# Two grouped attentions of a decoder: value products issued in pairs, output products two units behind

## The chip, the cores and the metric

The kernel runs on one core of a Trainium2 chip. The metric is the device time of one execution in microseconds; the profiler gives, for one execution, what each engine did and when. TensorE (PE) multiplies, with its weight loads shown apart (PEld); VectorE (DVE) and ScalarE (ACT) read and write both the accumulator banks (PSUM) and on-chip memory (SBUF); GpSimd (POOL) here splits weights; SyncE (SP) issues DMAs.

## What is computed

Two decoder layers with layer norms behind each block, on x of 16 x 64 tokens and 512 features, in float32. The change touches the two blocks with 32 heads of 128 and 8 key/value heads (four query heads share one):

```python
# block B: cross attention, layer 0: keys and values from ctx, rotary embedding, mask
q = rope(x @ Wq); k = rope(ctx @ Wk); v = ctx @ Wv
o = softmax(where(mask == 0, -1e9, q @ k.T / sqrt(128))) @ v
x = layernorm(x + o @ Wo)
# block D: self attention, layer 1: causal, window of 64
o = softmax(where(causal, q @ k.T / sqrt(128), -inf)) @ v
x = layernorm(x + o @ wo.T)
```

The blocks before, between and behind them (another attention, two feed-forward blocks, a single-head cross attention) are not changed.

## The kernel before, in words

Tokens lie in 8 tiles (NT) of 128, that is two batch rows of 64 each. `grouped_attention` (line 685) is called for B (line 1097, with rotation) and for D (line 1250, without). Either works through four parts; a part is a pair of key/value heads. A part has 16 units (SLOTS): unit u is token tile u % 8 with key/value head u // 8 of the pair, so it holds 2 batch rows x 4 query heads. The first three parts run in a hardware loop, the last one (`part.final`) is written out behind it. Each engine runs its own instruction stream; semaphores with running counts order them.

Matrix products with weights are made from high and low parts: `three` (line 88) gives high x high, high x low and low x high, and `product` (line 80) accumulates them in one bank. So each activation has to be split before it is multiplied: ScalarE writes the high part, VectorE subtracts it from the bank to get the low part.

On TensorE, slot u does in this order (`turn`, line 852):

- T(u): two transposes of unit u's probabilities into bankT (line 858), when VectorE has them ready (`prob`).
- S(u+2): scores of unit u+2 into a bankA (line 825). In late slots (u % 4 == 2) they come further back.
- O(u): the value product. Two matmuls of 64 rows, one for each batch row, into the two banks of bankO (line 870). The trace shows each as two passes, four in all. It waits for ScalarE's copy of T(u) (`pt_done`), for the values, and until bankO has been split for unit u-1 (`o_low`).
- Y(u-1): the output product of the unit before (`output`, line 828), 12 matmuls of 512 columns from oT, the split O, into a bankY. It waits for the low part of oT and for the bank. In late slots it stands ahead of O(u).
- Q(u+6): a query projection, 12 matmuls of 512 columns; in some slots a value projection V, and four key projections K in slot 13. A projection waits until its bankA is drained (in B: until the first rotation step of the query two banks before).
- at u % 8 == 7 also Y(u), its halves counted apart (`wo_used`).

On ScalarE, slot u copies T(u) to pt (line 959), in B copies the two halves of Q(u+5) swapped (line 910) and in D copies Q(u+5) itself (line 912), writes the high part of O(u) to oT (line 967), and then computes exp of unit u+2 (line 922); in late slots that exp comes in the slot behind. In slots of SPLIT_AT it also writes the high part of a weight block (line 937). In the final part it does the first `ln_roots` (line 111; the square roots of tiles 0 to 3, whose table has to be loaded) behind slot 14.

On VectorE, slot u interleaves (`in_turns`) the rotation of Q(u+5) in three steps (lines 1013, 1015, 1019; B alone), the front of the softmax of unit u+2 (lines 1026, 1030, 1033) and the back of unit u+1 (lines 1038, 1041, 1044). Then come the residual of u-2 (line 1049; in the final part with the layer norm's statistics, `ln_follow`), the low part of O(u) (line 1082) and the low part of a weight block (line 1060).

oT is kept twice, by u % 2, and bankO holds one unit in columns 0 to 255 of its two banks:

```python
oT = [[sb(mem, f"{tag}oT{i}{p}", [P, GROUP, 2, S], F32R) for p in range(2)] for i in range(2)]
...
act.wait_ge(o_ready, part.unit(u) + 1)
nc.scalar.activation(oT[u % 2][0][:].rearrange("p h b q -> p b h q"),
                     bankO[:, :, 0:GROUP * S].rearrange("p b (h q) -> p b h q", h=GROUP), ACT.Copy).then_inc(o_high, 1)
if not late(u) and (u + 2 < SLOTS or not part.final):
    exp(part, u + 2)
```

Of the kernel before, what the change touches and what calls it, by code (L numbers as in the profile page):

```python
# [42 lines left out]
def build_program(nc, io):  # L43
# [641 lines left out]
    def grouped_attention(tag, norm, first, source, rope, following):  # L685
# [6 lines left out]
        with ExitStack() as mem:  # L692
# [12 lines left out]
            oT = [[sb(mem, f"{tag}oT{i}{p}", [P, GROUP, 2, S], F32R) for p in range(2)] for i in range(2)]  # L705
# [13 lines left out]
            for i, (q, o) in enumerate(zip(halves(wq, "p h k n -> p (h k n)"), halves(wo, "p h n -> p (h n)"))):  # L719
                dst[f"q{i}"] = dst[f"q{i + 2}"] = q  # L720
                dst[f"o{i}"] = dst[f"o{i + 2}"] = o

# [7 lines left out]
            with nc.Block() as block:  # L730
# [30 lines left out]
                def _(pe):  # L761
# [67 lines left out]
                    def output(part, u):  # L829

                        if u % NT == 0:
                            pe.wait_ge(w_low, part.block("o3" if u else "o1"))
                        pe.wait_ge(o_low, part.unit(u) + 2)
                        pe.wait_ge(y_done, part.unit(u) + 1)
                        pairs = [x for h in range(GROUP) for x in three([o[:, h].rearrange("p b q -> p (b q)") for o in oT[u % 2]], [w[:, h, :] for w in wo])]
                        if u % NT == NT - 1:
                            product(bankY[u % 2][:], pairs[:len(pairs) // 2], stop=False).then_inc(wo_used, 1)
                            product(bankY[u % 2][:], pairs[len(pairs) // 2:], start=False).then_inc(y_ready, 1)
                        else:
                            product(bankY[u % 2][:], pairs).then_inc(y_ready, 1)  # L840

# [10 lines left out]
                    def turn(part):  # L852
                        for u in range(SLOTS):
                            banks = slot_banks(u, part.final)
                            pe.wait_ge(st["prob"], part.unit(u) + 1)
                            pe.wait_ge(pt_done, part.unit(u) + 1)
                            for hp in range(2):
                                done = nc.tensor.transpose(bankT[u % 2][:, hp * P:(hp + 1) * P], sc[u % 4][:, hp].rearrange("p b k -> p (b k)"), ident[:])  # L858
                            done.then_inc(t_ready, 1)
                            if banks and banks[0][0] == "S" and not late(u):  # L860
                                project(part, banks[0])
                            if late(u):
                                output(part, u - 1)
                            if u < NT and u % 2 == 0:
                                pe.wait_ge(v_done, part.it * 4 + u // 2 + 1)
                            pe.wait_ge(pt_done, part.unit(u) + 3)
                            pe.wait_ge(o_low, part.unit(u) + 1)
                            for b in range(2):
                                rows = slice(S * b, S * b + S)
                                done = nc.tensor.matmul(bankO[:, b, 0:GROUP * S], V[rows, u % NT, u // NT * HD:(u // NT + 1) * HD], pt[u % 2][rows, :], start=True, stop=True)  # L870
                            done.then_inc(o_ready, 1)
                            if u % NT and not late(u):
                                output(part, u - 1)
                            for x in banks:
                                if x[0] != "S" or late(u):
                                    project(part, x)
                            if u % NT == NT - 1:
                                output(part, u)
# [20 lines left out]
                def _(act):  # L899
# [50 lines left out]
                    def turn(part):  # L950
                        for u in range(SLOTS):
# [12 lines left out]
                            if len(banks) == 1:  # L964
                                queries_or_keys(part, banks[0])
                            act.wait_ge(o_ready, part.unit(u) + 1)
                            nc.scalar.activation(oT[u % 2][0][:].rearrange("p h b q -> p b h q"),  # L967
                                                 bankO[:, :, 0:GROUP * S].rearrange("p b (h q) -> p b h q", h=GROUP), ACT.Copy).then_inc(o_high, 1)
                            if not late(u) and (u + 2 < SLOTS or not part.final):
                                exp(part, u + 2)  # L970
                            if u in VALUES_AT and not part.final:
# [5 lines left out]
                            if part.final and u == SLOTS - 2:  # L977
                                ln_roots(act, norm + 1, 0)
# [5 lines left out]
                def _(dve):  # L984
# [85 lines left out]
                    def turn(part):  # L1070
                        for u in range(SLOTS):
# [7 lines left out]
                            if u % NT >= 2:  # L1079
                                residual(part, u - 2)  # L1080
                            dve.wait_ge(o_high, part.unit(u) + 1)
                            nc.vector.tensor_tensor(oT[u % 2][1][:].rearrange("p h b q -> p b h q"), bankO[:, :, 0:GROUP * S].rearrange("p b (h q) -> p b h q", h=GROUP),  # L1082
                                                    f32(oT[u % 2][0][:]).rearrange("p h b q -> p b h q"), ALU.subtract).then_inc(o_low, 1)
# [6 lines left out]
                            if u % NT == NT - 1:  # L1090
                                residual(part, u - 1)
# [612 lines left out]
```

## Time and profile before

| | |
|---|---|
| median of 3 runs | 1679.96 us (1678.95 to 1680.19) |
| the profiled execution | 1680.69 us, span 1678.9 us |
| mean granted TensorE clock | 0.984 of 2.4 GHz |
| TensorE busy | 1584.1 us (94% of the span), 8504 matmuls |
| VectorE busy | 983.7 us (59%) |
| ScalarE busy | 657.6 us (39%) |
| GpSimd busy | 202.6 us (12%) |
| block B | about 253 to 801 us |
| block D | about 900 to 1438 us |

Busy time of an engine says how full it is, not what waits for what; TensorE's idle time, and what ended it, shows that. In the rows, a line stands for a group of instructions: start, time, engine, line of the kernel, operation, out<-in, partitions x elements and count; in brackets the idle time of the engine before it and what ended it. Matmuls overlap, so the time from start to start is what one costs, and the time of one is longer.

### The profile page before, as it was taken

What the parts mean: (1) busy time and instruction counts of PE and PEld (TensorE: products, weight loads), DVE (VectorE), ACT (ScalarE), POOL (GpSimd) and SP (SyncE); (2) the same over time, 40 slices, a digit from 0 to 9 for tenths busy, and PEclk for the clock granted to TensorE, in tenths of its full rate; (3) what the DMA queues carried; (4) which work ended last, traced back from release to release, by engine and by line L of the source; (5) the groups of instructions that cost most, each with busy time, mean ns of one, the idle gap of its engine ahead of it and who ended that gap; (6) DMA issues with size and microseconds to landing.
All of it is one profiled execution on the core that took longest, in us unless ns stands there. A gap on an engine that the chain in (4) does not pass through costs nothing. (4 is left out here: it accounts for less than half of the span.)

```text
span 1678.9 us, 22758 instructions
## 1 busy us (share of the span) xinstructions
PE 1584.1 (94%) x8504; PEld 1269.8 (76%) x8504; DVE 983.7 (59%) x1948; ACT 657.6 (39%) x1193; POOL 202.6 (12%) x146
## 2 busy tenths in 40 slices
PE   8688799999999999999889999999999999989998
PEld 6566587787788778776777788788878877767876
DVE  5997767756766776677433542452553346246655
ACT  4476434333433443433233322332332323426541
POOL 8321130000000000000340000000000000703330
PEclk9899999999999999999999999999999999999999
DMA  6011011101110110100111110110110100202231
GB/s 229 30 38 40 15 49 63 51 13 39 38 51 2 63 51 13 39 13 26 45 52 38 41 48 13 50 51 12 50 60 15 38 13 25 77 10 77 77 90 50
DMA packets 26023, 75.44 MB, mean 45 GB/s; under 512 B 3888, under 2 KB 4624, under 8 KB 25680
## 3 DMA queue, kind: packets, MB, share of 16 engines
q1 hardware_dynamic: 25552, 73.16, 13.2%
q8 instruction: 63, 1.03, 0.2%
q0 software_dynamic: 384, 1.05, 0.2%
q14 instruction: 24, 0.20, 0.0%
HBM read 72.10 MB, written 2.10 MB: 44 GB/s over the span
## 5 line engine op out<-in xcount | busy, mean ns | idle before, releaser
L83 PE MATMUL bankY<-sb_Dwo,sb_DoT 128*128 128x512 f32 x768 | 194.0, 402 | 0.3 <-DVE sb_DoT L1082 0.3
L83 PE MATMUL bankY<-sb_Bwo,sb_BoT 128*128 128x512 f32 x768 | 193.0, 400 | 0.2 <-DVE sb_BoT L1082 0.2
L83 PE MATMUL bankA<-sb_xT,sb_Bwq 128*128 128x512 f32 x768 | 190.4, 397 | 0.9 <-issue 0.9
L83 PE MATMUL bankA<-sb_xT,sb_Dwq 128*128 128x512 f32 x768 | 189.9, 396 | 0.0
L83 PEld LDWEIGHTS bankY<-sb_Dwo,sb_DoT 128*128 128x128 f32 x768 | 141.0, 189 | 42.3 <-issue 13.3
L83 PEld LDWEIGHTS bankY<-sb_Bwo,sb_BoT 128*128 128x128 f32 x768 | 140.6, 189 | 42.0 <-issue 13.2
L83 PEld LDWEIGHTS bankA<-sb_xT,sb_Bwq 128*128 128x128 f32 x768 | 142.3, 188 | 35.2 <-issue 4.0
L83 PEld LDWEIGHTS bankA<-sb_xT,sb_Dwq 128*128 128x128 f32 x768 | 142.2, 188 | 34.0 <-issue 2.7
L1013 DVE TENSOR_TENSOR sb_BqT<-bankA,sb_Btable 128x512 f32<-128x512 f32 x64 | 44.3, 692 | 150.3 <-ACT sb_Bsw L910 150.3
L1049 DVE TENSOR_TENSOR sb_xtok<-sb_xtok,bankY 128x512 f32<-128x512 f32 x128 | 87.2, 681 | 54.0 <-PE bankY L83 53.9
L910 ACT ACTIVATE sb_Bsw<-bankA 64x512 f32<-64x512 f32 x160 | 94.7, 592 | 54.9 <-PE bankA L83 51.7
L1026 DVE TENSOR_TENSOR sb_Dsc<-bankA,sb_Dbound 128x256 f32<-128x256 f32 x64 | 27.0, 421 | 149.2 <-PE bankA L825 149.2
L1082 DVE TENSOR_TENSOR sb_DoT<-bankO,sb_DoT 128x512 fp32r<-128x512 f32 x64 | 43.8, 685 | 117.3 <-ACT sb_DoT L967 117.3
L959 ACT ACTIVATE sb_Dpt<-bankT 128x256 f32<-128x256 f32 x64 | 24.5, 382 | 155.2 <-PE bankT L858 155.2
L825 PE MATMUL bankA<-sb_Bkt,sb_BqT 128*128 128x128 f32 x512 | 69.3, 278 | 8.0 <-DVE sb_BqT L1019 7.8
L78 POOL TENSOR_TENSOR sb_Ew<-sb_raw,sb_zero 128x1024 fp32r<-128x1024 f32 x4 | 7.6, 1891 | 566.3 <-POOLq L730 566.3
L825 PEld LDWEIGHTS bankA<-sb_Bkt,sb_BqT 128*128 128x128 f32 x512 | 62.1, 191 | 14.3 <-DVE sb_BqT L1019 8.7
L922 ACT ACTIVATE sb_Bsc<-sb_Bsc 128x256 f32<-128x256 f32 x64 | 26.7, 416 | 115.5 <-DVE sb_Bsc L1033 115.5
L78 POOL TENSOR_TENSOR sb_Cwar<-sb_raw,sb_zero 128x1024 fp32r<-128x1024 f32 x1 | 1.9, 1892 | 575.8 <-POOLq L730 575.8
L825 PE MATMUL bankA<-sb_Dkt,sb_DqT 128*128 128x128 f32 x512 | 69.0, 278 | 0.0
L825 PEld LDWEIGHTS bankA<-sb_Dkt,sb_DqT 128*128 128x128 f32 x512 | 62.2, 191 | 5.1 <-issue 5.0
L967 ACT ACTIVATE sb_DoT<-bankO 128x512 fp32r<-128x512 f32 x64 | 38.3, 599 | 65.0 <-PE bankO L870 65.0
(277 smaller groups left out, 2968.2 us busy)
## 6 DMA issues: line engine op xcount, KB each, us to landing
sb_raw<-in_w_attn SPq DMA_DIRECT2D x80, 512.0 KB, 3.5
sb_raw<-in_q_gu SPq DMA_DIRECT2D x22, 256.0 KB, 2.7
sb_raw<-in_q_d SPq DMA_DIRECT2D x11, 256.0 KB, 2.7
sb_raw<-in_wqk SPq DMA_DIRECT2D x8, 256.0 KB, 2.6
sb_rawx<-in_xT SPq DMA_DIRECT2D x4, 512.0 KB, 5.7
sb_raw<-in_ctxT SPq DMA_DIRECT2D x4, 512.0 KB, 6.2
sb_xtok<-in_x_tok SPq DMA_DIRECT2D x1, 2048.0 KB, 13.1
sb_raw<-in_ctx_tok SPq DMA_DIRECT2D x4, 512.0 KB, 3.8
```

Of the source, the lines that this page charges most:

```text
L78: return nc.gpsimd.tensor_tensor(dst, src, zero[0:src.shape[0]].to_broadcast([src.shape[0], src.shape[1]]), ALU.add)
L83: last = nc.tensor.matmul(out, lhs, rhs, start=start and i == 0, stop=stop and i == len(pairs) - 1)
L825: done = nc.tensor.matmul(bank[:, at:at + P], qT[:, 2 * t + b, 2 * hp:2 * hp + 2, :].rearrange("p h q -> p (h q)"), window(kt, 2 * t + b, ...
L910: nc.scalar.activation(sw[part.swap(x)][64 * i:64 * i + 64, :], bankA[part.buffer(x)][64 - 64 * i:P - 64 * i, :], ACT.Copy).then_inc(swapp ...
L922: nc.scalar.activation(flat, flat, ACT.Exp, scale=HD ** -0.5).then_inc(st["exp"], 1)
L959: nc.scalar.activation(pt[u % 2][:], bankT[u % 2][:, 0:GROUP * S], ACT.Copy).then_inc(pt_done, 1)
L967: nc.scalar.activation(oT[u % 2][0][:].rearrange("p h b q -> p b h q"), bankO[:, :, 0:GROUP * S].rearrange("p b (h q) -> p b h q", h=GROUP ...
L1013: nc.vector.tensor_tensor(to, bankA[part.buffer(x)][:].rearrange("p (b s) -> p b s", s=S), table[:, 0, half].rearrange("p (b s) -> p b s", ...
L1026: nc.vector.tensor_tensor(s3, bankA[part.buffer(("S", u))][:].rearrange("p (a c) -> p a c", a=2)[:, :, S:S + P], bound_of(u).unsqueeze(1). ...
L1049: nc.vector.tensor_tensor(xtok[:, t, :], xtok[:, t, :], bankY[u % 2][:], ALU.add).then_inc(y_done, 1)
L1082: nc.vector.tensor_tensor(oT[u % 2][1][:].rearrange("p h b q -> p b h q"), bankO[:, :, 0:GROUP * S].rearrange("p b (h q) -> p b h q", h=GR ...
```

## The change

- The value products of two units are issued together, in odd slots: `attend(part, u)` makes O(u-1) and O(u) one behind the other, into columns 0 to 255 (even unit) and 256 to 511 (odd unit) of bankO's two banks. It waits for both copies of transposes and until the pair before has been split.
- oT holds one pair, [P, 2, GROUP, 2, S] for either part, instead of two units apart. One ScalarE instruction writes the high part of the pair and one VectorE instruction its low part (1024 columns instead of twice 512), in odd slots.
- The output product runs two units behind: Y(u-2) in slots with u % 8 >= 2, ahead of the pair's value products; Y(6) and Y(7) at the end of slot 7 (14 and 15 in slot 15). The residual runs three units behind.
- On ScalarE exp(u+2) stands ahead of the high part of O, not behind it.
- In the last slot of the final part the pair is split unit by unit, and Y(13) comes behind the value products. The first `ln_roots` moves from the end of slot 14 to behind the high part of unit 14, ahead of that of unit 15.

```diff
@@ -702,7 +702,7 @@
             V = sb(mem, f"{tag}V", [P, NT, 2 * HD])
             sc = [sb(mem, f"{tag}sc{i}", [P, 2, 2, S]) for i in range(4)]
             pt = [sb(mem, f"{tag}pt{i}", [P, GROUP * S]) for i in range(2)]
-            oT = [[sb(mem, f"{tag}oT{i}{p}", [P, GROUP, 2, S], F32R) for p in range(2)] for i in range(2)]
+            oT = [sb(mem, f"{tag}oT{p}", [P, 2, GROUP, 2, S], F32R) for p in range(2)]
             mx = sb(mem, f"{tag}mx", [P, 2, 4]); sm = sb(mem, f"{tag}sm", [P, 2, 4]); ri = sb(mem, f"{tag}ri", [P, 2, 4])
             if rope:
                 sw = [sb(mem, f"{tag}sw{i}", [P, HALF]) for i in range(2)]
@@ -719,6 +719,18 @@
             for i, (q, o) in enumerate(zip(halves(wq, "p h k n -> p (h k n)"), halves(wo, "p h n -> p (h n)"))):
                 dst[f"q{i}"] = dst[f"q{i + 2}"] = q
                 dst[f"o{i}"] = dst[f"o{i + 2}"] = o
+
+            def side(v):
+                return slice(v % 2 * GROUP * S, (v % 2 + 1) * GROUP * S)
+
+            def of_pair(i):
+                return oT[i][:].rearrange("p v h b q -> p b (v h) q")
+
+            def of_unit(i, v):
+                return oT[i][:, v % 2].rearrange("p h b q -> p b h q")
+
+            pair_bank = bankO[:].rearrange("p b (h q) -> p b h q", q=S)
+            unit_bank = lambda v: bankO[:, :, side(v)].rearrange("p b (h q) -> p b h q", q=S)
 
             def run(engine, start, turn):
 
@@ -832,12 +844,24 @@
                             pe.wait_ge(w_low, part.block("o3" if u else "o1"))
                         pe.wait_ge(o_low, part.unit(u) + 2)
                         pe.wait_ge(y_done, part.unit(u) + 1)
-                        pairs = [x for h in range(GROUP) for x in three([o[:, h].rearrange("p b q -> p (b q)") for o in oT[u % 2]], [w[:, h, :] for w in wo])]
+                        pairs = [x for h in range(GROUP) for x in three([o[:, u % 2, h].rearrange("p b q -> p (b q)") for o in oT], [w[:, h, :] for w in wo])]
                         if u % NT == NT - 1:
                             product(bankY[u % 2][:], pairs[:len(pairs) // 2], stop=False).then_inc(wo_used, 1)
                             product(bankY[u % 2][:], pairs[len(pairs) // 2:], start=False).then_inc(y_ready, 1)
                         else:
                             product(bankY[u % 2][:], pairs).then_inc(y_ready, 1)
+
+                    def attend(part, u):
+
+                        if u < NT:
+                            pe.wait_ge(v_done, part.it * 4 + u // 2 + 1)
+                        pe.wait_ge(pt_done, part.unit(u) + 3)
+                        pe.wait_ge(o_low, part.unit(u))
+                        for v in (u - 1, u):
+                            for b in range(2):
+                                rows = slice(S * b, S * b + S)
+                                done = nc.tensor.matmul(bankO[:, b, side(v)], V[rows, v % NT, v // NT * HD:(v // NT + 1) * HD], pt[v % 2][rows, :], start=True, stop=True)
+                            done.then_inc(o_ready, 1)
 
                     def start(part):
                         if rope:
@@ -859,22 +883,18 @@
                             done.then_inc(t_ready, 1)
                             if banks and banks[0][0] == "S" and not late(u):
                                 project(part, banks[0])
-                            if late(u):
-                                output(part, u - 1)
-                            if u < NT and u % 2 == 0:
-                                pe.wait_ge(v_done, part.it * 4 + u // 2 + 1)
-                            pe.wait_ge(pt_done, part.unit(u) + 3)
-                            pe.wait_ge(o_low, part.unit(u) + 1)
-                            for b in range(2):
-                                rows = slice(S * b, S * b + S)
-                                done = nc.tensor.matmul(bankO[:, b, 0:GROUP * S], V[rows, u % NT, u // NT * HD:(u // NT + 1) * HD], pt[u % 2][rows, :], start=True, stop=True)
-                            done.then_inc(o_ready, 1)
-                            if u % NT and not late(u):
-                                output(part, u - 1)
+                            ending = part.final and u == SLOTS - 1
+                            if u % NT >= 2 and not ending:
+                                output(part, u - 2)
+                            if u % 2:
+                                attend(part, u)
+                            if ending:
+                                output(part, u - 2)
                             for x in banks:
                                 if x[0] != "S" or late(u):
                                     project(part, x)
                             if u % NT == NT - 1:
+                                output(part, u - 1)
                                 output(part, u)
                     run(pe, start, turn)
                     ln_tensor(pe, norm + 1, EARLY)
@@ -963,19 +983,24 @@
                                 exp(part, u + 1)
                             if len(banks) == 1:
                                 queries_or_keys(part, banks[0])
-                            act.wait_ge(o_ready, part.unit(u) + 1)
-                            nc.scalar.activation(oT[u % 2][0][:].rearrange("p h b q -> p b h q"),
-                                                 bankO[:, :, 0:GROUP * S].rearrange("p b (h q) -> p b h q", h=GROUP), ACT.Copy).then_inc(o_high, 1)
                             if not late(u) and (u + 2 < SLOTS or not part.final):
                                 exp(part, u + 2)
+                            if part.final and u == SLOTS - 1:
+                                act.wait_ge(o_ready, part.unit(u) + 1)
+                                nc.scalar.activation(of_unit(0, u - 1), unit_bank(u - 1), ACT.Copy).then_inc(o_high, 1)
+                                ln_roots(act, norm + 1, 0)
+                                act.wait_ge(y_ready, part.unit(u - 2) + 1)
+                                act.wait_ge(o_low, part.unit(u - 1) + 2)
+                                nc.scalar.activation(of_unit(0, u), unit_bank(u), ACT.Copy).then_inc(o_high, 1)
+                            elif u % 2:
+                                act.wait_ge(o_ready, part.unit(u) + 1)
+                                nc.scalar.activation(of_pair(0), pair_bank, ACT.Copy).then_inc(o_high, 2)
                             if u in VALUES_AT and not part.final:
                                 values(part, VALUES_AT[u])
                             if u in SPLIT_AT:
                                 weights_high(part, SPLIT_AT[u])
                             for x in projected_last(u, part.final):
                                 queries_or_keys(part, x)
-                            if part.final and u == SLOTS - 2:
-                                ln_roots(act, norm + 1, 0)
                             if part.final and u == SLOTS - 1:
                                 ln_rest(act, norm + 1)
                     run(act, start, turn)
@@ -1076,11 +1101,15 @@
                             in_turns(rotate(part, *banks) if rope and banks else None,
                                      None if late(u) else scores,
                                      back(part, u + 1) if u + 1 < SLOTS or not part.final else None)
-                            if u % NT >= 2:
-                                residual(part, u - 2)
-                            dve.wait_ge(o_high, part.unit(u) + 1)
-                            nc.vector.tensor_tensor(oT[u % 2][1][:].rearrange("p h b q -> p b h q"), bankO[:, :, 0:GROUP * S].rearrange("p b (h q) -> p b h q", h=GROUP),
-                                                    f32(oT[u % 2][0][:]).rearrange("p h b q -> p b h q"), ALU.subtract).then_inc(o_low, 1)
+                            if u % NT >= 3:
+                                residual(part, u - 3)
+                            if part.final and u == SLOTS - 1:
+                                for v in (u - 1, u):
+                                    dve.wait_ge(o_high, part.unit(v) + 1)
+                                    nc.vector.tensor_tensor(of_unit(1, v), unit_bank(v), f32(of_unit(0, v)), ALU.subtract).then_inc(o_low, 1)
+                            elif u % 2:
+                                dve.wait_ge(o_high, part.unit(u) + 1)
+                                nc.vector.tensor_tensor(of_pair(1), pair_bank, f32(of_pair(0)), ALU.subtract).then_inc(o_low, 2)
                             if u % NT == 0:
                                 weights_low(part, "o3" if u else "o1")
                             if u in SPLIT_AT:
@@ -1088,6 +1117,7 @@
                             if late(u):
                                 in_turns(scores)
                             if u % NT == NT - 1:
+                                residual(part, u - 2)
                                 residual(part, u - 1)
                                 if rope:
                                     in_turns(rotate(part, *projected_last(u, part.final)))
```

## Rows read from the trace of the kernel before

**Rows 1.** Stretches B, D: us, busy PE, PEld, DVE, ACT, POOL, PEclk, DMA share, GB/s.

```profile
253.00:801.00 548.00, 533.20 (x2793) 427.35 (x2793) 377.75 (x776) 220.50 (x393) 0.02 (x1) 1.00 0.11 35
...
900.00:1438.00 538.00, 533.37 (x2795) 427.64 (x2793) 249.99 (x564) 173.83 (x321) 0.00 (x0) 1.00 0.11 35
```

**Rows 2.** Groups by line and shape: busy us, mean ns, idle before, releasers.

```profile
L825 PE MATMUL bankA<-sb_Bkt,sb_BqT 128*128 128x128 f32 x512 | 69.3, 278 | 8.0 <-DVE sb_BqT L1019 7.8 <-DVE sb_BqT L1013 0.2
...
L870 PE MATMUL bankO<-sb_Bpt,sb_BV 64*128 64x256 f32 x256 | 45.5, 432 | 4.6 <-ACT sb_Bpt L959 3.6 <-DVE sb_BoT L1082 1.0
...
L870 PE MATMUL bankO<-sb_Dpt,sb_DV 64*128 64x256 f32 x256 | 45.0, 428 | 3.0 <-ACT sb_Dpt L959 3.0
...
L83 PE MATMUL bankY<-sb_Bwo,sb_BoT 128*128 128x512 f32 x768 | 193.0, 400 | 0.2 <-DVE sb_BoT L1082 0.2
...
L83 PE MATMUL bankY<-sb_Dwo,sb_DoT 128*128 128x512 f32 x768 | 194.0, 402 | 0.3 <-DVE sb_DoT L1082 0.3
```

**Rows 3.** TensorE's timeline, one D unit: start, us, ..., [idle]; last, second half of 907.25.

```profile
906.04 0.38 PE L858 MATMUL bankT<-sb_ident,sb_Dsc 128*128 128x128 f32 x2
906.26 1.06 PE L825 MATMUL bankA<-sb_Dkt,sb_DqT 128*128 128x128 f32 x8
907.25 0.70 PE L870 MATMUL bankO<-sb_Dpt,sb_DV 64*128 64x256 f32 x4
907.88 3.03 PE L83 MATMUL bankY<-sb_Dwo,sb_DoT 128*128 128x512 f32 x12
910.75 2.96 PE L83 MATMUL bankA<-sb_xT,sb_Dwq 128*128 128x512 f32 x12
913.55 0.38 PE L858 MATMUL bankT<-sb_ident,sb_Dsc 128*128 128x128 f32 x2
...
907.57 0.38 PE L870 MATMUL bankO<-sb_Dpt,sb_DV 64*128 64x256 f32 x2
```

**Rows 4.** Timeline of TensorE, B, units 1 and 2 of a part.

```profile
404.37 0.38 PE L858 MATMUL bankT<-sb_ident,sb_Bsc 128*128 128x128 f32 x2
...
411.85 0.38 PE L858 MATMUL bankT<-sb_ident,sb_Bsc 128*128 128x128 f32 x2
411.99 3.01 PE L83 MATMUL bankY<-sb_Bwo,sb_BoT 128*128 128x512 f32 x12
...
416.19 1.16 PE L825 MATMUL bankA<-sb_Bkt,sb_BqT 128*128 128x128 f32 x8 [0.56 <-DVE sb_BqT L1019]
```

**Rows 5.** Timeline of ScalarE and VectorE, B, the same units.

```profile
406.43 0.69 DVE L1013 TENSOR_TENSOR sb_BqT<-bankA,sb_Btable 128x512 f32<-128x512 f32 x1 [1.35 <-ACT sb_Bsw L910]
...
409.69 0.42 DVE L1044 TENSOR_TENSOR sb_Bsc<-sb_Bsc,sb_Bri 128x256 f32<-128x256 f32 x1
...
409.80 0.42 ACT L922 ACTIVATE sb_Bsc<-sb_Bsc 128x256 f32<-128x256 f32 x1 [2.78 <-DVE sb_Bsc L1033]
...
410.13 1.04 ACT L937 ACTIVATE sb_Bwq<-sb_raw 128x1024 fp32r<-128x1024 f32 x1
...
411.20 1.23 DVE L1060 TENSOR_TENSOR sb_Bwq<-sb_raw,sb_Bwq 128x1024 fp32r<-128x1024 f32 x1 [0.50 <-ACT sb_Bwq L937]
```

**Rows 6.** Timeline, the end of D.

```profile
1424.96 1.28 ACT L111 ACT_TABLE_LOAD   x1
...
1426.87 0.70 PE L870 MATMUL bankO<-sb_Dpt,sb_DV 64*128 64x256 f32 x4 [2.21 <-ACT sb_Dpt L959]
...
1427.50 7.39 PE L83 MATMUL bankY<-sb_Dwo,sb_DoT 128*128 128x512 f32 x24
...
1428.11 2.92 ACT L117 ACTIVATE sb_xtok<-sb_xtok,sb_ln_offset,sb_ln_rstd 128x512 f32<-128x512 f32 x4
...
1434.73 1.04 PE L168 MATMUL bankT<-sb_ident,sb_xtok 128*128 128x128 f32 x8
...
1437.33 0.55 DVE L148 TENSOR_SCALAR sb_xtok<-sb_xtok,sb_ln_rstd,sb_ln_offset 128x512 f32<-128x512 f32 x1
```

**Rows 7.** One stretch of the end of D, columns as in rows 1.

```profile
1429.00:1431.00 2.00, 2.00 (x6) 1.54 (x6) 0.00 (x0) 2.00 (x4) 0.00 (x0) 0.50 0.00 0
```

## The prediction, made before the change was timed

> **What bounds the kernel now.** I read first the busy time of the two stretches that the change touches, the cross attention B and the windowed attention D: TensorE is busy for 533.2 of 548 us and 533.4 of 538 us, VectorE for 378 and 250 us [rows 1]. So TensorE's order of work is the time in both, and VectorE has little room in B and much in D. The groups by line show what TensorE waits for: 7.8 us for rotated queries in B, 4.6 and 3.0 us in all before value products, 0.2 and 0.3 before output products [rows 2]. Then the timeline of one ordinary D unit [rows 3], of units 1 and 2 of a part in B on TensorE [rows 4] and on ScalarE and VectorE [rows 5], and of the last units [rows 6]. There the last value product waits 2.21 us for a copy that is queued behind the table load and the square root. The granted clock of one stretch there is in [rows 7].
>
> **Part 1, pairing the value products.** In [rows 3] eight 128-column passes start at 906.26 and the value product at 907.25: 0.99 us where eight at the pace of 0.11 take 0.89, so 0.10 to enter. The product holds TensorE 0.63 us (907.25 to 907.88); its second half starts 0.32 after the first. The following twelve take 2.87 us, the next twelve 2.80; twelve at 0.23 are 2.77, so leaving costs 0.10 more. A pass of 256 columns at the pace above would take 0.22, two of them 0.43: 0.20 of the 0.63 is weight loading at entry and running empty at the exit. One product in the middle of others thus costs 0.83, of which 0.40 is changing over. Paired, the second product costs between 0.43 (only streaming) and 0.63 (as now). I take 0.43, since the 0.32 between the halves is 0.11 of first load plus 0.21, the streaming alone, and a load behind a running pass is hidden everywhere in [rows 3]. 64 pairs x 0.40 = **-25.6 us** (lower bound of the gain 64 x 0.20 = 12.8).
>
> The Trainium skill (TensorEngine Tiling (Array Packing), Key Properties) says that changing the tiling mode drains TensorE. The 0.10, 0.20 and 0.10 agree with it.
>
> **Part 2, one split for both.** The ScalarE copy of 1024 columns takes 1.04 us and the VectorE subtraction 1.22, as the weight blocks of that size do [rows 5]. With three handovers of somewhat under 0.1 the pair's low part is there 2.5 us after the second product. It is less busy time than before, but one later, longer chain, and in ScalarE's order exp(u+2) now stands ahead of the copy, so the copy waits for VectorE's softmax of unit u+2.
>
> **Part 3, what the output product now waits for.** It stands at u-2: at units 1 and 9 there is none, and at unit 2 (10) output(0) needs the pair of units 0 and 1. Count from the transposes of unit 1 in B (404.37) by [rows 4, 5]. VectorE's first rotation step of Q6 ends at +2.75 and frees the bank that Q7 needs; TensorE is ready at 0.22+0.98+0.63+0.43 = 2.26, since output(0) no longer stands between: 0.55 idle. Probabilities of unit 2 are done at +5.74, TensorE ready at 5.68: 0.1. exp(3) runs +5.43 to 5.85, so the pair's copy ends at 6.80 and the subtraction at 8.05; output(0) starts at 8.1 where it could at 6.0: **2.1 idle**. VectorE then has the low part of a weight block (1.2) and Q7's rotation (2.2) before S(4): +11.6, output(0) being over at 11.05: 0.6. That is 3.35 us idle at unit 1 and at unit 9: 8 halves x 3.35 = +26.8. In D there is no rotation: its three steps of 0.7 [rows 5], of which 0.1 lies under the next, are gone from ahead of exp(3), which is over 1.9 us earlier, and the same count leaves 0.25 x 8 = +2.0.
>
> The scores of unit 8 (in slot 6) come at a fixed 4.34 us after the transposes, as at unit 2 (411.85 to 416.19), through copy, swap and rotation, whatever TensorE does meanwhile. The value product that stood there (0.83) is gone, so the 0.6 wait grows to 1.3: 4 x 1.3 = +5.2. By the same chain output(6), now directly behind Q13, waits 0.55 in four parts (+2.2), and the scores of unit 16 wait 0.5 in three (+1.5). The first slot of B, whose Q6 waits for VectorE anyway, gives nothing back: +0.8. The waits that these replace go: 12 in late slots, 0.56 idle and the 0.07 beside it each [rows 4], in all -7.6 of the 7.8 [rows 2].
>
> **Part 4, the last units of B and D.** No projections are left there. At unit 12 only transposes and scores (1.1 us) stand between the pair (10, 11) and output(10), which needs 2.5: 1.35 idle; at unit 14 the transposes alone (0.22): 2.25; at unit 15 the products wait for the copy of their transposes: 0.6. Together +4.2 each, **+8.4**. What stood there goes: the waits at units 11, 12, 14 and 15, in B 1.0 for the low part and 2.2 for the copy before value products, 0.2 before an output product; in D 2.2 and 0.3 [rows 2, 6]: -5.9, D's first product's 0.8 being handed on to the next transposes, which wait for VectorE instead. After the 2.21 wait TensorE ran at a granted clock of 0.50 (1.2 GHz) [rows 7]: 24 output matmuls took 7.23 us (1427.50 to 1434.73) instead of 5.6 [rows 6]; I take 1.5 each: -3.0.
>
> Roots behind the last product: the table load (1.28) and root (0.30) no longer stand ahead of the transposes' copy [rows 6], they lie beside output(13). But tiles 0 to 3 are normalised only after residual(13), which comes behind both last splits, some 3 us later; that pushes the roots and scalings of the groups behind it. Before, the last normalisation ends 3.4 us after output(15) (1434.73 to 1437.88 and its hand-over); worked out with the 4 scalings (2.92 [rows 6]) that would now start 8.2 us after unit 15's transposes, then a root, 2 scalings and the last group, it becomes 4.45: +1.05 x 2 = +2.1.
>
> SyncE and GpSimd: no DMA is added, loads follow the low parts of the weights and have microseconds to spare; no work moves past them. oT needs half the memory, no time.
>
> **Sum.** New waits: 26.8+2.0+5.2+2.2+1.5+0.8+8.4+2.1 = +49.0. Gone: 25.6+7.6+5.9+3.0 = -42.1. Net +6.9 on the profiled execution's 1680.69 (span 1678.9): 1687.6; the median shown is 0.7 lower, so 1686.9. Ten of the new waits are about as long as the one in [rows 6], after which the clock fell. If it falls after two of them, at 1.2 each (a part is absorbed by the wait for S(4)), it is **1689**.
>
> **Rivals.**
> (a) Faster: the cross attention's queue doesn't bind. Mechanism: the pair's copy and subtraction finish under Q7, as they nearly do in D by the count above, and only the saved change-overs count. Place: unit 1 and 9 in B; price: without the 35.7 us of B's waits (26.8+5.2+2.2+1.5), 1651. It decides once B's new waits are under 29 us. For it: VectorE is idle 170 of 548 us in B [rows 1]. Against it: exp(3) starts at 409.80, 5.4 us after the transposes, and the copy is behind it in ScalarE's order. The rule of the Trainium skill named above (TensorEngine Tiling (Array Packing), Key Properties), taken alone, gives this way: half as many changes of mode, so faster. 8%.
> (b) The second product of a pair costs what the first does, 0.63. That adds 0.20 x 64 = 12.8, of which some 3.5 fall into waits: 1698. Against it: the halves' distance. 12%.
> (c) The clock falls at nearly all ten long waits, 8 x 1.0 + 2 x 1.5 = +11: 1698. For it: it fell after the 2.21 wait [rows 6, 7]. Against it: that wait stood between short products and transposes, while twelve full matmuls stand on either side of the new ones. 18%.
> (d) The forecast, 62%.
>
> **How the numbers follow.** The forecast's own range is 1682 to 1694: of 49 us of waits, eight counts of the same chain at unit 1 carry 27, and 0.1 us on the copy or subtraction moves the sum by about 1.5, 0.3 by 4 to 5. The range for 8 in 10 reaches to (b) and (c): 1681 to 1699. A measurement here can tell about 0.2% (3.4 us) from no change. Faster than 1676.6: (a) and a tail of the forecast, 0.09. Between 1676.6 and 1683.3: the lower edge of the forecast, 0.12. Slower: 0.79.
>
> **What would show it.** In the changed kernel's timeline: the value products as groups of 8, about 1.06 us long (1.26 would be (b)); a pair's copy of about 1.04 and subtraction of about 1.22; TensorE idle before output matmuls for the low part of oT, about 2.1 us at units 2 and 10 of B and 0.25 in D; waits for rotated queries grown from 7.8 to over 15 us; the stretch of D some 10 us shorter and that of B some 17 longer. No wait for the copy of the transposes behind the table load. Wrong if B's stretch grows by less than 8 us, if the idle time at unit 2 is under 1 us, or if a wait appears on a weight block.

## The result, and the profile after

The changed kernel takes 1700.7 us (median of 4 runs, 1700.1 to 1705.1), the kernel before 1679.84 (4 runs, 1678.95 to 1680.19): a ratio of 1.0125, interval 1.0113 to 1.0137. It is slower, as forecast, but by 20.9 us where the forecast had 9, and 1.7 us beyond the end of the range. The profiled execution took 1700.43 us, span 1698.5, mean granted clock 0.977 (before 0.984).

First the two stretches of [rows 1], from the same events to the same events, in the columns of [rows 1].

```profile
253.00:827.00 574.00, 537.45 (x2795) 432.20 (x2793) 380.44 (x748) 212.26 (x361) 0.00 (x0) 0.98 0.10 34
926.00:1456.00 530.00, 521.88 (x2796) 426.91 (x2794) 250.52 (x533) 168.29 (x290) 0.00 (x0) 1.00 0.11 36
```

B is 26 us longer and D 8 shorter. In B TensorE's busy time grew by 4 us although change-overs were removed, and the mean clock fell to 0.98: idle time and a slower clock both have a share. The groups by line and shape of the changed kernel (busy us, mean ns, idle before and its releasers) say where TensorE now stands idle.

```profile
L83 PE MATMUL bankY<-sb_Bwo,sb_BoT 128*128 128x512 f32 x768 | 199.8, 413 | 20.7 <-issue 15.7 <-DVE sb_BoT L1112 5.0
L83 PE MATMUL bankY<-sb_Dwo,sb_DoT 128*128 128x512 f32 x768 | 190.1, 398 | 4.2 <-DVE sb_DoT L1112 3.4
L837 PE MATMUL bankA<-sb_Bkt,sb_BqT 128*128 128x128 f32 x512 | 69.3, 279 | 7.6 <-DVE sb_BqT L1044 5.8 <-DVE sb_Bkt L1044 1.6 <-DVE sb_BqT L1038 0.2
L863 PE MATMUL bankO<-sb_Bpt,sb_BV 64*128 64x256 f32 x256 | 36.3, 402 | 0.5 <-ACT sb_Bpt L979 0.5
L863 PE MATMUL bankO<-sb_Dpt,sb_DV 64*128 64x256 f32 x256 | 36.3, 402 | 0.5 <-ACT sb_Dpt L979 0.5
```

Against [rows 2]: the value products wait 0.5 us in a block where they waited 4.6 and 3.0, and are busy 9 us less in each block; B's output products wait 20.7 us where they waited 0.2, and a single one of their matmuls takes 413 ns on average against 398 in D. Eight of these waits, 15.7 us in all and 2.0 at most, are put down to "issue".

TensorE's timeline of B, the units of [rows 4] (start, us, engine, line, operation, tiles, number, [idle before]):

```profile
411.24 0.38 PE L882 MATMUL bankT<-sb_ident,sb_Bsc 128*128 128x128 f32 x2
411.46 1.06 PE L837 MATMUL bankA<-sb_Bkt,sb_BqT 128*128 128x128 f32 x8
412.45 1.13 PE L863 MATMUL bankO<-sb_Bpt,sb_BV 64*128 64x256 f32 x8
414.06 3.04 PE L83 MATMUL bankA<-sb_xT,sb_Bwq 128*128 128x512 f32 x12 [0.47 <-DVE sb_BqT L1038]
417.04 0.44 PE L882 MATMUL bankT<-sb_ident,sb_Bsc 128*128 128x128 f32 x2
419.44 4.57 PE L83 MATMUL bankY<-sb_Bwo,sb_BoT 128*128 128x512 f32 x12 [1.96 <-issue]
423.85 0.38 PE L837 MATMUL bankA<-sb_Bkt,sb_BqT 128*128 128x128 f32 x2
```

Timeline of ScalarE and VectorE for the same units, as in [rows 5]:

```profile
416.68 0.42 ACT L942 ACTIVATE sb_Bsc<-sb_Bsc 128x256 f32<-128x256 f32 x1 [3.40 <-DVE sb_Bsc L1058]
417.00 1.00 ACT L997 ACTIVATE sb_BoT<-bankO 128x1024 fp32r<-128x1024 f32 x1
...
418.11 1.23 DVE L1112 TENSOR_TENSOR sb_BoT<-bankO,sb_BoT 128x1024 fp32r<-128x1024 f32 x1 [1.13 <-ACT sb_BoT L997]
```

The pair's value products are over at 413.5, but ScalarE takes exp(3) first, at 416.68, 5.44 us after the transposes, and the copy behind it. The subtraction ends at 419.34 and output(0) starts at 419.44: TensorE has stood still since 417.48. "Issue" is this same wait for the low part of oT, though the view doesn't name it: all eight are 1.96 us long, and each ends 0.1 us after a subtraction has. And the twelve matmuls behind it take 4.41 us (419.44 to 423.85) where [rows 3] have 2.87. The granted clock says why; two windows of the changed kernel, columns as in [rows 1]:

```profile
417.00:419.50 2.50, 0.54 (x4) 0.29 (x3) 1.39 (x2) 2.48 (x5) 0.00 (x0) 1.00 0.00 0
419.50:423.00 3.50, 3.50 (x10) 2.75 (x11) 3.44 (x7) 0.94 (x2) 0.00 (x0) 0.58 0.34 117
```

The clock is full (2.4 GHz) up to the wait's end and 0.58 on the mean behind it: most of that stretch ran at 1.2 GHz. Distances from one unit's transposes to the next ones', worked out from the two timelines for the second part of B, units 0 to 15, show which units pay for it:

```
before  5.39 7.48  8.13 7.50 7.49 7.49 8.12 10.26 4.72 7.48 11.01 7.49 10.35 18.38 10.35 13.10
after   4.00 5.80 10.50 7.91 6.66 7.89 8.14 14.04 3.91 5.80 13.37 7.89  9.52 18.81 10.32 16.47
```

Unit 2 is 10.50 in the first two parts and 9.53 and 9.58 in the other two; unit 10 is 13.37 in three parts and 7.70 in the last; unit 14 of the last parts is 7.04 (B) and 7.02 (D). So the clock fell at eight of the ten long waits: twice at unit 2, four times at unit 10, twice at unit 14. Against the same units with the clock full (9.53 at unit 2 here; 12.39 and, in the last part, 6.13 at unit 10 in experiment 3) a fall costs 1.0 us at each of five places and 1.6 at the last unit 10. At the two units 14 no run has the full clock; an estimate (the output product starts 2.58 us behind the transposes, and twelve matmuls at full clock take 2.8) makes them 5.4, and the fall some 1.7 each. That is 9.8 us in all, against some 3, by the prediction's count, that the kernel before had lost in the same way at its two units 15.

In D nothing of the kind happens in the looped parts. TensorE there, units 1 and 2 of the first part (the last row output(0)):

```profile
931.83 1.06 PE L837 MATMUL bankA<-sb_Dkt,sb_DqT 128*128 128x128 f32 x8
932.82 1.13 PE L863 MATMUL bankO<-sb_Dpt,sb_DV 64*128 64x256 f32 x8
933.88 3.05 PE L83 MATMUL bankA<-sb_xT,sb_Dwq 128*128 128x512 f32 x12
936.77 0.38 PE L882 MATMUL bankT<-sb_ident,sb_Dsc 128*128 128x128 f32 x2
937.26 2.97 PE L83 MATMUL bankY<-sb_Dwo,sb_DoT 128*128 128x512 f32 x12
```

The pair lasts 1.06 us (932.82 to 933.88), and output(0) comes 0.27 us after the transposes are through (936.77 + 0.22). At the end of D, however, both waits of the last units are there:

```profile
1434.16 0.44 PE L882 MATMUL bankT<-sb_ident,sb_Dsc 128*128 128x128 f32 x2
1436.74 4.60 PE L83 MATMUL bankY<-sb_Dwo,sb_DoT 128*128 128x512 f32 x12 [2.14 <-DVE sb_DoT L1112]
1441.18 0.38 PE L882 MATMUL bankT<-sb_ident,sb_Dsc 128*128 128x128 f32 x2
1442.04 1.14 PE L863 MATMUL bankO<-sb_Dpt,sb_DV 64*128 64x256 f32 x8 [0.47 <-ACT sb_Dpt L979]
```

The 2.21 us of [rows 6] have become 0.47, but a wait of 2.14 stands one unit earlier in the order of work, and the clock falls behind that one instead (4.60 us for twelve matmuls).

Where the 19.6 us of span went, from the starts of the blocks' parts in both traces: B's three looped parts +19.4 (145.78, 144.76, 144.74 before; 153.25, 151.04, 150.44 after), B's last part +5.5 up to its last transposes, its tail up to the last tiles' layer norm +1.0, D's looped parts -8.4, D's last part -1.0, its tail +0.9. The rest, 2.2, lies in stretches whose code the change leaves alone: 0.8 ahead of B, -0.4 between the blocks, 1.8 behind D.

The 1.8 behind D is a fall of the clock too. TensorE waits there for the last tiles' layer norm, 1.80 us before and 2.93 after, because the norm is over later. The 10 us from that wait's end, first in the kernel before and then in the changed one, columns as in [rows 1]:

```profile
1438.40:1448.40 10.00, 7.88 (x41) 6.32 (x42) 4.88 (x8) 4.71 (x9) 9.81 (x5) 1.00 0.20 63
1456.20:1466.20 10.00, 8.55 (x32) 6.87 (x33) 4.88 (x8) 4.67 (x9) 9.79 (x5) 0.66 0.19 65
```

All of the 1.8 us is lost in these 10 us. In every run with pairs in D's last part (the change, experiments 1, 2 and 3) the wait is 2.93 and the clock 0.66 behind it, at 1.5 to 1.9 us; in the five others the wait is 1.80, the clock 1.00, and nothing is lost.

### The profile page after: what moved, and what is told of

Its sections match the earlier page's. It is cut to its first block and busy times, and to the rows that moved or that the text cites. A ratio compares the mean times of both kernels' runs of the same rounds, so it can differ in the third digit from the quotient of the medians.

```text
span 1698.5 us, 22696 instructions
## 1 busy us (share of the span) xinstructions
PE 1578.9 (93%) x8504; PEld 1276.9 (75%) x8504; DVE 985.5 (58%) x1886; ACT 644.3 (38%) x1131; POOL 202.1 (12%) x146
## 3 DMA queue, kind: packets, MB, share of 16 engines
q0 software_dynamic: 384, 1.05, 0.2%
## 5 line engine op out<-in xcount | busy, mean ns | idle before, releaser
L83 PE MATMUL bankY<-sb_Bwo,sb_BoT 128*128 128x512 f32 x768 | 199.8, 413 | 20.7 <-issue 15.7
L83 PE MATMUL bankY<-sb_Dwo,sb_DoT 128*128 128x512 f32 x768 | 190.1, 398 | 4.2 <-DVE sb_DoT L1112 3.4
L83 PEld LDWEIGHTS bankY<-sb_Bwo,sb_BoT 128*128 128x128 f32 x768 | 147.5, 197 | 55.3 <-issue 17.7
L1112 DVE TENSOR_TENSOR sb_DoT<-bankO,sb_DoT 128x1024 fp32r<-128x1024 f32 x31 | 38.0, 1225 | 65.2 <-ACT sb_DoT L997 65.2
L979 ACT ACTIVATE sb_Bpt<-bankT 128x256 f32<-128x256 f32 x64 | 24.5, 383 | 103.8 <-PE bankT L882 103.7
```

Source lines behind the costliest of these rows:

```text
L83: last = nc.tensor.matmul(out, lhs, rhs, start=start and i == 0, stop=stop and i == len(pairs) - 1)
L979: nc.scalar.activation(pt[u % 2][:], bankT[u % 2][:, 0:GROUP * S], ACT.Copy).then_inc(pt_done, 1)
L1112: nc.vector.tensor_tensor(of_pair(1), pair_bank, f32(of_pair(0)), ALU.subtract).then_inc(o_low, 2)
```

## The experiments

The kernels of the experiments hold both forms of the code behind switches (`paired`, the order on ScalarE, the place of the roots); the diffs below show what a setting comes to.

**1. The copy ahead of exp.** The theory: the order on ScalarE makes the wait at output(0) and output(8), and the wait makes the clock fall. Only that order is turned, in both blocks.

```diff
-                            if not late(u) and (u + 2 < SLOTS or not part.final):
-                                exp(part, u + 2)
                             if part.final and u == SLOTS - 1:
...
                             elif u % 2:
                                 act.wait_ge(o_ready, part.unit(u) + 1)
                                 nc.scalar.activation(of_pair(0), pair_bank, ACT.Copy).then_inc(o_high, 2)
+                            if not late(u) and (u + 2 < SLOTS or not part.final):
+                                exp(part, u + 2)
```

> The changed kernel with one order undone: on ScalarE the pair's high part of O comes ahead of exp(u+2) again. My theory: at units 1 and 9 of B the pair's chain is queued behind exp(u+2), which costs 2.1 us of waiting at output(0) and output(8), and the long wait then lets the clock fall (1.0 us more in 6 of the 8 places, 1.7 in the last part). With the copy first, TensorE's wait at the output product of units 2 and 10 in B is under 0.9 us, the clock stays up there, B's loop gets 2.4 us shorter per part by the shorter chain and 1 to 2 by the clock: the whole kernel 14 to 19 us faster than the changed one, 1682 to 1687. Rival (the loss is the pairing or the two-unit distance itself, whatever the order on ScalarE): within 3 us of 1700.7.

Measured: 1681.62 us (10 runs, 1678.56 to 1683.87) against 1680.1 before, ratio 1.0009 (0.9999 to 1.0019): 19 us of the change's 20.9 are gone; the time is 0.4 below the expected range. Timelines of this kernel in the second part of B, TensorE (`product` is line 89 here, the pair line 886), then ScalarE and VectorE:

```profile
407.28 0.39 PE L905 MATMUL bankT<-sb_ident,sb_Bsc 128*128 128x128 f32 x2
...
408.49 1.13 PE L886 MATMUL bankO<-sb_Bpt,sb_BV 64*128 64x256 f32 x8
...
413.08 0.44 PE L905 MATMUL bankT<-sb_ident,sb_Bsc 128*128 128x128 f32 x2
414.26 3.00 PE L89 MATMUL bankY<-sb_Bwo,sb_BoT 128*128 128x512 f32 x12 [0.74 <-issue]
417.89 1.16 PE L845 MATMUL bankA<-sb_Bkt,sb_BqT 128*128 128x128 f32 x8 [0.63 <-DVE sb_BqT L1086]
```

```profile
409.73 1.03 ACT L1033 ACTIVATE sb_BoT<-bankO 128x1024 fp32r<-128x1024 f32 x1 [0.41 <-PE bankO L886]
...
412.72 0.42 ACT L975 ACTIVATE sb_Bsc<-sb_Bsc 128x256 f32<-128x256 f32 x1 [1.97 <-DVE sb_Bsc L1100]
...
412.94 1.22 DVE L1157 TENSOR_TENSOR sb_BoT<-bankO,sb_BoT 128x1024 fp32r<-128x1024 f32 x1
```

The copy is over at 410.76, 2 us before exp(3) begins. What is left, 0.74, is VectorE's: its queue has softmax work ahead of the subtraction, which starts only at 412.94. Unit 2 takes 8.61 us (10.50 with the change), unit 10 11.48 (13.37), in every looped part, and the twelve matmuls take 3.00 us: in the looped parts there is no wait of 2 us and no fall of the clock. The order on ScalarE is shown to be the cause of most of the loss: from its first to its last transposes B was 24.9 us longer than before with the change and is 7.6 longer here, and D gains another 2.8. B's looped parts are still 6.1 us longer than before in sum and D's 10.4 shorter, so pairing still loses in B. No experiment takes this remainder apart; of TensorE's waits in B, those for rotated queries before scores are 10.5 us in this run (7.8 before), those at output(0) and output(8) 5.9.

**2. The change in D alone.** Pairs, output two behind and late roots in D; B as before.

```diff
+            paired = lambda part: not rope
```

(`rope` is true in B; where `paired` is false, value product, split, output and roots go as before the change.)

> The change in block D alone; block B runs as before, with the roots at their old place. Theory: D gains 2.8 us per part in its loop (8 pairs x 0.41 less waits) and 1 in the last part, its tail is 0.9 longer: 8 to 9 us faster than before, 1671 to 1673, give or take 2 for where the clock falls in the norms. Rival (the second product of a pair costs as much as a single one): 5 us less gain, 1676 to 1678.

Measured: 1672.82 us (4 runs) against 1680.1, ratio 0.9956 (0.9939 to 0.9972): 7.3 us faster, inside the expected times. The looped parts of D take 140.70, 139.73 and 139.73 us (143.41, 142.54 and 142.54 before). The change is a gain in the block where the counts of the prediction gave one.

**3. Work in the gap.** If the clock costs something of its own, idle matmuls in the wait should make the kernel faster, though they only add work. Eight go ahead of output(0) and output(8) in B, 64 in all, into a transposes' bank that nothing reads then.

```diff
+                            if rope and u % NT == 2:
+                                product(bankT[(u + 1) % 2][:], [(xT[0][:, 0, 0:P], xT[0][:, 0, 0:HALF])] * 8)
                             if u % NT >= 2 and not ending:
                                 output(part, u - 2)
```

> The changed kernel with 8 idle matmuls of 512 columns more on TensorE ahead of output(0) and output(8) in B, 1.85 us, put into the wait of 2.1 us (they write a bank of bankT that nobody reads then). They take no time from the chain. Theory (the clock falls because of that wait, 1.04 us in 6 places and 1.7 in the last part): with the wait filled the clock does not fall there, slots 2 and 10 last 9.4 to 9.6 and 12.3 to 12.4 us in all parts, and the kernel is 5 to 8 us faster than the changed one, 1693 to 1696, though it does 64 matmuls more. Rival (the longer slots have another cause, or the clock is not worth anything there since the chain on VectorE decides): 1700 or slower.

Measured: 1693.99 us (4 runs, 1691.74 to 1694.68), 6.7 us faster than the change with 64 matmuls more. TensorE's timeline, the third row the idle matmuls, and a window behind the wait with the columns of [rows 1]:

```profile
414.36 0.44 PE L905 MATMUL bankT<-sb_ident,sb_Bsc 128*128 128x128 f32 x2
414.55 2.07 PE L89 MATMUL bankT<-sb_xT 128*128 128x512 f32 x8
416.76 3.01 PE L89 MATMUL bankY<-sb_Bwo,sb_BoT 128*128 128x512 f32 x12
```

```profile
419.00:423.00 4.00, 3.67 (x21) 2.86 (x20) 2.82 (x8) 0.00 (x0) 0.00 (x0) 1.00 0.39 124
```

The twelve matmuls take 3.01 us instead of 4.57. Unit 2 is 9.51 to 9.56 in all four parts (10.50 where the clock had fallen, 9.53 and 9.58 where it hadn't), unit 10 is 12.39 three times and then 6.13 (13.37 and 7.70). So the fall costs 1.0 us at a looped unit and 1.6 in the last part. Where the clock hadn't fallen the idle matmuls change nothing: unit 2 is as long with them as without.

**4. The roots alone.** The kernel before, with the first groups' roots moved to behind the copy of unit 15's value product; nothing paired.

```diff
-                            if part.final and u == SLOTS - 2:
-                                ln_roots(act, norm + 1, 0)
                             if part.final and u == SLOTS - 1:
+                                ln_roots(act, norm + 1, 0)
                                 ln_rest(act, norm + 1)
```

> The kernel before with the first square roots moved alone: behind the high part of unit 15 in the last part of B and D. Theory: the last value product no longer waits 2.2 us behind the table load (about 1.2 us remain, for the bank of unit 14 to be split), the clock does not fall there, but the normalisation of tiles 0 to 3 starts later: 0.7 us gained in each block by the order and up to 1.5 by the clock: 1676 to 1679. Rival (the tail of the norm gives all of it back): 1679.5 to 1680.5.

Measured: 1678.75 us (10 runs, 1677.13 to 1680.43) against 1680.1, ratio 0.999 (0.9981 to 1.0). Inside what can be told from no change, and the sign is as expected. The end of D in its timeline:

```profile
1426.87 0.70 PE L870 MATMUL bankO<-sb_Dpt,sb_DV 64*128 64x256 f32 x4 [1.14 <-DVE sb_DoT L1150]
1427.51 3.02 PE L89 MATMUL bankY<-sb_Dwo,sb_DoT 128*128 128x512 f32 x12
1428.23 1.28 ACT L117 ACT_TABLE_LOAD   x1
```

The wait of 2.21 [rows 6] is 1.14, now for the low part of unit 14, and the first twelve matmuls behind it take 3.02 us: after this shorter wait the clock stays up. The table load is hidden beside them. In the profiled execution the tails of B and D, from the last transposes to the last tiles' norm, are 1.9 and 2.0 us shorter than before, where 0.7 by the order and up to 1.5 by the clock had been worked out; between B's norm and D's start 1.6 us of it is lost again, where the kernel ran 13.7 us at 1.2 GHz and the kernel before 6.8.

**5. Pairs where they pay.** Pairs with the copy first in D's looped parts, everything else single, roots late in both blocks.

```diff
+            paired = lambda part: not rope and not part.final
```

> A version put together from what the runs showed: block B as before, block D in pairs in its three looped parts only, with the pair's copy ahead of exp(u+2), single products in the last parts, and the first square roots at their late place in both blocks. Theory: 3.2 us per looped part of D from the pairing, in the last part and the norms what the roots alone brought (1.4): 1668 to 1670. Rival (the gain of D's pairs is tied to the order on ScalarE of the changed kernel): 1672 or slower.

Measured: 1667.12 us (5 runs, 1666.36 to 1669.5) against 1680.5, ratio 0.9922 (0.9908 to 0.9935): 13.4 us faster than before, 33.6 faster than the change, and 0.9 below the expected range. It beats both kernels. D's looped parts take 140.04, 139.11 and 139.03 us; the groups by line of this kernel show output products that hardly wait:

```profile
L89 PE MATMUL bankY<-sb_Bwo,sb_BoT 128*128 128x512 f32 x768 | 192.4, 399 | 0.6 <-DVE sb_BoT L1150 0.6
...
L89 PE MATMUL bankY<-sb_Dwo,sb_DoT 128*128 128x512 f32 x768 | 189.8, 397 | 0.6 <-DVE sb_DoT L1150 0.6
```

**6. The change in B alone.** The counterpart of experiment 2: D as before, its roots at the old place.

```diff
+            paired = lambda part: rope
```

> The change in block B alone; block D as before with its roots at the old place. Theory: the two blocks add up, B costs all of the loss and what D gives back besides: 1700.7 - 1679.9 + 7.3 = 28 us slower than before, 1706 to 1711. Rival (the blocks do not add up, e.g. the clock): below 1704.

Measured: 1706.28 us (4 runs) against 1680.5, ratio 1.0157 (1.0141 to 1.0172): 25.8 us slower. With D's -7.3 that makes 18.5 of the whole change's 20.9; the blocks add up to within 2.4 us. Unit 10 is 13.37 to 13.38 again, unit 2 is 9.51, 9.50, 10.48 and 9.59: this time the clock fell at unit 2 in one part, not two.

**7. Singles in the last parts.** The change, but without pairs in the last part of each block.

```diff
+            paired = lambda part: not part.final
```

> The changed kernel with single value products, one unit behind, in the last part of B and of D (roots late there). Theory: this takes away the waits of 1.35, 2.25 and 0.6 us of either last part and the slow clock behind them, and in B one wait of 2.1 with its clock; O(15)'s shorter wait comes back: slots 10 to 15 of the last parts some 3 us shorter in each block, B's last part without the slow slot 10, 1688 to 1693 in all. Rival (the last parts' loss is the roots' place): 1697 or slower.

Measured: 1686.69 us (4 runs, 1684.36 to 1689.98), ratio 1.0043 (1.0028 to 1.0059): 14 us faster than the change, and 1.3 below the expected range. Its last part of B takes 98.43 us to the last transposes (103.91 with the change, 98.42 before) and D's 95.19 (94.33 and 95.29). In the profiled execution (1684.36, the fastest of the four and 16.1 below the changed kernel's) B's last part gives 5.5 us, the stretch behind D's last transposes 4.6 (252.7 for 257.3; experiments 4 and 5, whose D ends in the same way, have 252.5 and 252.6; 1.8 of the 4.6 is the fall of the clock behind the norm), the looped parts of B 2.1, of which one fall of the clock fewer explains half, and the stretch between B's and D's transposes 4.4, while D's last part costs 0.9 more. Of those 4.4, 3.5 belong to no edit: in experiments 4 and 5 the same end of B and the same code up to D take 113.2 us, here 109.7. The granted clock differs there: between B's norm and D's start TensorE ran at 1.2 GHz for 13.7 us in experiments 4 and 5 (0.93 on the mean) and for 3.4 here (0.98). So with the same code a longer time at 1.2 GHz goes with 3.5 us more in that stretch; why the clock fell more often in one execution than in another stays open.

## Why the prediction was right and wrong

- **Part 1 held.** A pair takes 1.06 us, so the second product costs 0.43 and rival (b), 1.26, is out. The Trainium skill (TensorEngine Tiling (Array Packing), Key Properties) has changes of tiling mode drain TensorE; the trace agrees, a change less per pair being worth 0.40 us. Taken alone that rule gave rival (a), and in D it comes out that way (-7.3 us, experiment 2); in B what stands behind the products decides.
- **Part 2 held**: copy 1.00, subtraction 1.23.
- **Part 3 held in D and, the clock apart, in B,** but for one sign. D's looped parts came out 2.7 to 2.8 us shorter each, as the counts have it. In B output(0) starts 8.20 us after unit 1's transposes, worked out as 8.1; its idle time 1.96, worked out as 2.1. Experiment 1 shows that the order on ScalarE is what makes it. The sign that failed: the waits for rotated queries and keys in B were to grow from 7.8 to over 15 us; they are 12.1 (5.8, 4.5, 1.6 and 0.2), since the scores of unit 4 wait 0.4 and not 0.6, and not at all where the clock has fallen, and those of unit 8 wait 1.05 and not 1.3.
- **Part 4 held but for one term.** The unit-14 wait is 2.14 (worked out 2.25) and that of unit 15 0.47 (0.6); the last normalisation comes 4.5 us after output(15) (worked out 4.45). Yet "-3.0" for the clock was given back at once: it fell at unit 14 instead, in both blocks. And the later norm, priced at +1.05 a block, let the clock fall behind it in D (1.8 us), for which the sum has no term.
- **The failed step is the one after the sum: "If it falls after two of them, at 1.2 each".** It fell after eight of ten, and the cost was 9.8 us in place of 2.4. That is rival (c), given 18%. Its argument against, that twelve full matmuls stand on either side of the new waits, was wrong: the clock fell at 1.96 us of idle time between such matmuls. Its price was nearly right (1.0 at looped units, as it said; 1.6 to 1.7 in last parts for 1.5). With the fall behind D's norm the clock's term is 11.6: 6.9 + 11.6 makes 18.5 of the profiled executions' 19.7, and 0.8 of the remaining 1.2 lies ahead of B.

The range ended at rival (c) with no room behind it, and the 1.8 behind D and the 0.8 ahead of B then carried the time past it. The way that the time moved was forecast for the right reason, the copy queued behind exp(u+2): that was no luck.

## What to carry to other kernels

When a wait of about 2 us is about to be created in front of TensorE, price its idle time and, as a second term, the matmuls behind it at half clock. Here the second cost 11.6 us, of which the kernel before had some 3 at its own waits. Count every wait that grows, those in the norm behind the block too. Before pairing two operations so that one split serves both, look at what stands ahead of the split on each queue that it passes: here one exp, which was not urgent, stood ahead of the copy. And judge a change block by block: the same edit was worth -7.3 us in D and +25.8 in B, and applied only where it pays it beat both kernels.

## What the runs showed that was not expected

- Idle time of 1.96 us on TensorE between full matmuls was enough for the granted clock to fall; 1.25 (unit 12 of the last parts), 1.14 (experiment 4) and 0.74 (experiment 1) were not. In the last units 2.14 us for VectorE's subtraction did the same, and behind D's norm 2.93 us in four runs of four, 1.80 in none of five. Eight idle matmuls in the gap kept it up, a net 6.7 us.
- The same wait does not always bring the fall, though all eight in B were 1.96 us long. At unit 10 it did every time; at unit 2 in two parts of four with the change, in one of four in experiment 6, and in one of the three paired parts in experiment 7. What tells these apart stays open.
- "Issue" as a releaser hid a wait on a semaphore: 15.7 us of B's output waits bore that label, while the subtraction that they waited for ended 0.1 us before each start. Idle matmuls in the same place took the label away with the gap.
